# The mean of a group norm moved from the pixels into the biases of the products behind it

## The reference

```
x = x + attention(gn(x))     # 12 heads of 32, each pixel sees a 7x7 window and 16 registers
x = x + experts(gn(x))       # router over 4 experts, top 2, each 384 -> 96 -> 384 with gelu

gn(v):  g = v in 32 groups of 12 channels;  (g - mean) / sqrt(var + 1e-5), over all pixels of an image
attention(x): q, k, v = x @ qkv_w.T + qkv_b;  reg_k, reg_v = registers @ qkv_w[384:].T + qkv_b[384:]
              softmax(q . [k of the window, reg_k] / sqrt(32)) @ [v, reg_v] @ out_w.T + out_b
experts(x):   probs = softmax(x @ router_w.T + router_b), two largest, made to sum to 1 (weights c_e)
              sum over e of c_e * (gelu(x @ fc1_w[e].T + fc1_b[e]) @ fc2_w[e].T + fc2_b[e])
```

## Time and profile before

| | |
|---|---|
| median of 3 runs | 627.7 us (627.43 to 632.37) |
| profiled execution | 630.17 us, of which the span 628.4 |
| mean granted TensorE clock | 0.992 |
| instructions | 22407 |
| matmuls on TensorE | 9227 |
| VectorE, ScalarE, GpSimd instructions | 1009, 609, 427 |

### The profile page before, as it was taken

One profiled execution on the slowest core, in us unless ns is written; L12 is line 12 of the kernel. 1 busy time (PEld: TensorE's weight loads), 2 busy tenths in 40 slices (PEclk: granted clock), 3 DMA queues, 4 the chain that ended last, 5 costly groups with the idle time before them and its releaser, 6 DMA issues.

```text
span 628.4 us, 22407 instructions
## 1 busy us (share of the span) xinstructions
PE 564.3 (90%) x9227; PEld 389.5 (62%) x9227; DVE 449.1 (71%) x1009; ACT 307.5 (49%) x609; POOL 292.0 (46%) x427
## 2 busy tenths in 40 slices
PE   3668789999998999898899998997988899998998
PEld 2337666676765766566666776656666556665554
DVE  6885676886887689775778887875687797773233
ACT  1763455224643488523453246531786438644321
POOL 3106774372814856429573546325676322313131
PEclk9999999999999999899999999998998999999999
DMA  8869769794369852597537964588440001211212
GB/s 308 189 148 288 197 176 267 208 267 125 94 149 228 241 135 61 129 246 220 133 89 184 279 173 133 127 217 229 129 135 25 2 35 42 77 40 38 76 44 108
DMA packets 130637, 94.11 MB, mean 150 GB/s; under 512 B 67132, under 2 KB 124392, under 8 KB 130536
## 3 DMA queue, kind: packets, MB, share of 16 engines
q1 hardware_dynamic: 121896, 77.39, 46.3%
q0 software_dynamic: 8640, 15.30, 8.0%
HBM read 56.29 MB, written 35.54 MB: 146 GB/s over the span
## 4 chain that ended last, share of the span: by engine, by line
PE 60%; DVE 18%; DMA 7%; issue 6%; ACT 5%; SPq 2%; POOL 1%; ACTq 0%; DVEq 0%; POOLq 0%
PE ps L1168 41%; PE ps L1351 7%; PE ps L1328 4%; PE ps L1302 4%; DVE MX L675 3%; DMA QS<-MT 3%; DVE ST L459 2%; DMA KB<-kscr 2%; DVE ON L695 1%; DVE SUMT L688 1%; DVE RINV L694 1%; SPq L262 1%; DVE X L562 1%; DVE KT L537 1%; DMA X<-in_x 1%
## 5 line engine op out<-in xcount | busy, mean ns | idle before, releaser
L1168 PE MATMUL ps<-XH,WQ 128*128 128x384 f16 x810 | 148.5, 333 | 14.5 <-DVE XH L508 8.2
L675 DVE TENSOR_REDUCE MX<-ps 128x2 f32<-128x372 f32 x216 | 107.8, 538 | 36.5 <-PE ps L1302 34.5
L1168 PEld LDWEIGHTS ps<-XH,WQ 128*128 128x128 f16 x810 | 76.9, 99 | 68.9 <-issue 12.6
L983 ACT ACTIVATE PT<-ps 128x448 f32<-128x448 f32 (+1 forms) x162 | 78.9, 509 | 49.2 <-PE ps L1328 49.0
L439 POOL TENSOR_TENSOR KT<-QS,KT 128x384 f16<-128x384 f32 x36 | 34.3, 963 | 95.2 <-ACT KT L1081 95.2
L1302 PE MATMUL ps<-KB,QS 120*32 120x186 f16 x1728 | 63.5, 247 | 12.6 <-issue 3.6
L1328 PE MATMUL ps<-QS,KB 122*128 122x112 f16 (+1 forms) x864 | 61.0, 212 | 9.7 <-DMA QS<-MT 5.2
L1168 PE MATMUL ps<-WQ,XH 128*128 128x128 f16 x972 | 61.8, 221 | 4.0 <-issue 4.0
L1168 PE MATMUL ps<-OS,WO 128*128 128x384 f16 x324 | 61.7, 326 | 2.3 <-DVE X L551 1.5
L380 POOL DMA_DIRECT2D QS<-MT x72 | 38.2, 535 | 51.0 <-ACT MT L973 48.9
L1168 PEld LDWEIGHTS ps<-WQ,XH 128*128 128x128 f16 x972 | 55.3, 99 | 10.0 <-issue 7.8
(11 more groups left out here) (167 smaller groups left out, 971.9 us busy)
## 6 DMA issues: line engine op xcount, KB each, us to landing
KB<-kscr SPq DMA_DIRECT2D x108, 192.0 KB, 4.2
kscr<-KT SPq DMA_DIRECT2D x72, 192.0 KB, 2.6
VR<-vscr SPq DMA_DIRECT2D x216, 56.0 KB
QS<-qscr SPq DMA_DIRECT2D x108, 96.0 KB, 5.3
X<-in_x SPq DMA_DIRECT2D x12, 576.0 KB, 5.4
out<-X SPq DMA_DIRECT2D x11, 576.0 KB, 3.3
qscr<-QT POOLq DMA_DIRECT2D x18, 192.0 KB, 3.9
qscr<-PT POOLq DMA_DIRECT2D x18, 192.0 KB, 5.3
```

The lines of the kernel that those rows point to most:

```text
L675: V.tensor_reduce(out=MX[:, s % 2, t, 2 * pair:2 * pair + 2], in_=ps[:, S_BANK(s, i), 0:2 * RUN].rearrange("p (h n) -> p h n", h=2), op=AL ...
L983: A(PTS[n % 4][:, 0:w], ps[:, ST_BANK(n), 0:w], ACT.Exp, scale=SCORE).then_inc(s_["exd"], 1)
L1168: last = mm(bank, lhsT(a, k), rhs(b, k), start=(k == 0 and n == 0), stop=(finish and k == steps - 1 and n == 2))
```

## The change

The first half becomes x * rstd, without nb: the mean is no longer taken out of the pixels. Since every product behind the norm is linear, the missing part is a constant for each output channel, nb passed through the weights, and it is added to the biases instead:

- `normalised` on VectorE and the blocks for k = 2 on ScalarE go. The second half is x * rstd minus the first half, in one VectorE instruction (`scalar_tensor_tensor`). For n = 1 and 2, GpSimd keeps k = 0 alone, with two instructions (a scaling into GT_ and a subtraction); VectorE takes k = 1 and 2, in each column for the strip of the column before, and in column 5 for strip 5 too.
- GpSimd makes `shifted_registers(n)`: registers minus nb, with nb as a 17th column, in halves (four small operations). The registers are shifted the other way, since the key and value biases that they are given hold the shift for pixels.
- `registers(i)` now runs for both images, i = 0 to 5, and has 36 products: register keys with the key shift (17 columns), query shift and value shift (one column each), register values. i = 3 to 5 stand at the end of the queries phase of stage 2. New biases BQ, the value bias BVX and from it obx are made by VectorE (`bias_columns`, `value_columns`, `output_bias`); `value_bias` runs again in stage 3.
- The gelu bias is FBX, made from `hidden_shift` (27 products of one column, stage 5 and expert part); the router's bias gets `logit_shift` (9 products).
- To have nb earlier, the group means of stages 2 and 5 move from behind queries 2 to behind queries 1, `parameters`, `deviation` and `more_parameters` one step each.
- `register_values(gi)`, two transfers on GpSimd's queue, moves from behind the query outputs to ahead of them.

The diff, cut to its core (the first `low_half` is the one of GpSimd, the second the one of VectorE):

```diff
-POOL_K = ((), (0, 1, 2), (0, 1, 2), ())
+POOL_K = ((), (0,), (0,), ())
...
             def low_half(n, blk, k):
...
+                link(nc.gpsimd.tensor_scalar(tmp, x_block(n, blk, k), cols["rstd"][:, k:k + 1], None, ALU.mult))
                 pool.wait_ge(s_["gn_hi"], n * GN_STEPS + blk * KC + k + 1)
-                nc.gpsimd.tensor_tensor(xh_block(n, blk, 1, k), tmp_block(n, k), xh_block(n, blk, 0, k), ALU.subtract
-                                        ).then_inc(s_["gn_lo_p"], 1)
+                nc.gpsimd.tensor_tensor(xh_block(n, blk, 1, k), tmp, xh_block(n, blk, 0, k), ALU.subtract).then_inc(s_["gn_lo_p"], 1)
+
+            def shifted_registers(n):
+                pool.wait_ge(s_["gn_par"], n + 1)
...
+                nc.gpsimd.tensor_tensor(RGF[:, :, 0:REGS], cols["regs"].rearrange("p (k n) -> p k n", n=REGS),
+                                        cols["nb"].unsqueeze(2).broadcast_to([P, KC, REGS]), ALU.subtract)
+                link(nc.gpsimd.tensor_copy(RGF[:, :, REGS:RCOLS], cols["nb"].unsqueeze(2)))
+                link(nc.gpsimd.tensor_copy(RG[:, 0, :, :], RGF[:, :, :]))
+                nc.gpsimd.tensor_tensor(RG[:, 1, :, :], RGF[:, :, :], RG[:, 0, :, :], ALU.subtract).then_inc(s_["rg"], 1)
...
             for gi in range(STAGES):
+                if gi:
+                    register_values(gi)
                 for s in range(TILES):
                     queries_out(gi, s)
-                if gi:
-                    register_values(gi)
+                    if gi in (2, 5) and s == 4:
+                        shifted_registers(gi // KC + 1)
...
-                V.tensor_scalar(tmp_block(n, k), x_block(n, blk, k), cols["rstd"][:, k:k + 1], cols["nb"][:, k:k + 1],
-                                ALU.mult, ALU.add).then_inc(s_["gn_t"], 1)
...
             def low_half(n, blk, k):
-                V.tensor_tensor(xh_block(n, blk, 1, k), tmp_block(n, k), xh_block(n, blk, 0, k), ALU.subtract).then_inc(s_["gn_lo_v"], 1)
+                dve.wait_ge(s_["gn_hi"], n * GN_STEPS + blk * KC + k + 1)
+                V.scalar_tensor_tensor(out=xh_block(n, blk, 1, k), in0=x_block(n, blk, k), scalar=cols["rstd"][:, k:k + 1],
+                                       in1=xh_block(n, blk, 0, k), op0=ALU.mult, op1=ALU.subtract).then_inc(s_["gn_lo_v"], 1)
...
                     reciprocals(gi, 4)
                     if n:
-                        normalised(n, s, 0)
+                        low_halves(n, s - 1)
                     if more:
                         keys_low(gi + 1, 3)
+                    normalise(gi, 4)
                     if n:
-                        normalised(n, s, 1)
-                    normalise(gi, 4)
+                        low_halves(n, s)
...
-                    if gi in (2, 5) and s == 2:
+                    if gi in (2, 5) and s == 1:
                         parameters(gi // KC + 1, 0)
-                    if gi in (2, 5) and s == 4:
+                    if gi in (2, 5) and s == 3:
                         more_parameters(gi // KC + 1)
...
+                if gi == 2:
+                    bias_columns(1, 0, KC)
+                    value_columns(1)
+                    for i in range(KC, 2 * KC):
+                        register_low(i)
...
-                A(xh_block(n, blk, 0, k), x_block(n, blk, k), ACT.Identity, bias=cols["nb"][:, k:k + 1],
+                A(xh_block(n, blk, 0, k), x_block(n, blk, k), ACT.Identity, bias=cols["zero"],
...
+            def registers(i):
+                img, g = divmod(i, KC)
+                pe.wait_ge(s_["rg"], img + 1)
                 pe.wait_ge(s_["wlo"], g + 1)
...
+                split_product(ps[:, 0, at:at + RCOLS], lambda a, k: WQ[:, g, a, k, P:2 * P], lambda b, k: RG[:, b, k, :])
+                split_product(ps[:, 0, at + RCOLS:at + RCOLS + 1], lambda a, k: WQ[:, g, a, k, 0:P], shift)
+                split_product(ps[:, 0, at + RCOLS + 1:at + RCOLS + 2], lambda a, k: WQ[:, g, a, k, 2 * P:3 * P], shift)
+                split_product(ps[0:REGS, 0, at + 32:at + 32 + P], lambda a, k: RG[:, a, k, 0:REGS], lambda b, k: WQ[:, g, b, k, 2 * P:3 * P]
+                              ).then_inc(s_["kr_mm"], 1)
...
-                    if gi == 0:
-                        pe.wait_ge(s_["kr_lo"], KC)
-                        pe.wait_ge(s_["vr_sb"], KC)
+                    if gi in (0, 2) and i == 3:
+                        pe.wait_ge(s_["kr_lo"], KC * (gi // 2 + 1))
+                        pe.wait_ge(s_["vr_sb"], KC * (gi // 2 + 1))
+                        pe.wait_ge(s_["bvlo"], gi // 2 + 1)
...
-                    if gi in (2, 5) and s == 2:
+                    if gi in (2, 5) and s == 1:
                         group_means(gi // KC + 1, 0)
...
+                if gi == 2:
+                    for i in range(KC, 2 * KC):
+                        registers(i)
+                if gi == KC:
+                    value_bias(1)
+                if gi == 5:
+                    hidden_shift(0, 0, 0)
```

More of the change, by code:

```diff
@@ new lines, in low_halves, with bias_columns, value_columns @@
+            def low_halves(n, blk):
+                for k in range(KC):
+                    if k not in POOL_K[n]:
+                        low_half(n, blk, k)
+            def bias_columns(img, first, end):
+                dve.wait_ge(s_["kr_mm"], KC * img + end)
+                V.tensor_tensor(BQ[:, img, first:end, :], regs_ps[:, first:end, REGS:REGS + 2],
+                                cols["qkb16"].rearrange("p (g t) -> p g t", t=2)[:, first:end, :], ALU.add).then_inc(s_["bq"], 1)
+            def value_columns(img):
+                link(V.scalar_tensor_tensor(out=BVX[:, :], in0=regs_ps[:, :, REGS + 2], scalar=1 / WS, in1=cols["bv"],
+                                            op0=ALU.mult, op1=ALU.add))
+                link(V.tensor_copy(BVH[:, 0, :], BVX[:, :]))
+                V.tensor_tensor(BVH[:, 1, :], BVX[:, :], BVH[:, 0, :], ALU.subtract).then_inc(s_["bvlo"], 1)
@@ L820, in result @@
                                        op0=ALU.mult, op1=ALU.add).then_inc(s_["y_done"], 1)
-            def last_values(blk):
-                for k in range(2):
-                    normalised(3, blk, k)
             def last_lows(blk):
@@ L888, in _ @@
             weigh(15)
-            last_values(5)
             weigh(16)
@@ L999, in _ @@
                     if gi == 0:
-                        for k in range(2):
+                        for k in range(KC):
                             normalised(0, a, k)
-                        if dve_lows(0, a) > 0:
-                            act.wait_ge(s_["gn_lo_v"], dve_lows(0, a))
-                        A(tmp_block(0, 2), x_block(0, a, 2), ACT.Identity, bias=cols["nb"][:, 2:3], scale=cols["rstd"][:, 2:3]).then_inc(s_["gn_ta"], 1)
-                        normalised(0, a, 2)
                         if a == 0:
@@ L1204, in value_bias, with hidden_shift, logit_shift @@
                 last.then_inc(s_["bv_mm"], 1)
+            def hidden_shift(img, bank, at):
+                pe.wait_ge(s_["rg"], img + 3)
+                pe.wait_ge(s_["flo"], 1)
+                for j in range(KC):
+                    last = split_product(ps[:, bank, at + j:at + j + 1], lambda a, k: W1[:, a, k, j * P:(j + 1) * P], shift)
+                last.then_inc(s_["fb_mm"], 1)
+            def logit_shift():
+                split_product(ps[:, 5, RSPAN:RSPAN + EXPERTS], lambda a, k: shift(a, k).broadcast_to([P, P]), lambda b, k: RWs[:, b, k, :])
```

242 lines of the change are left out of this document (120 added, 122 removed).

## The result

The changed kernel took 644.5 us (median of four runs, 641.0 to 647.7), the one before 628.6 beside it: ratio 1.027, interval 1.021 to 1.032. That is slower by some 16 us, where 636.6 with a range of 629.5 to 643 was forecast: the sign is right, the size too small by half. The execution shown here is the fastest of the four, 641.01 us with 639.2 of span.

A forecast was written before the change was run, and what follows sets the result against it. The prediction took TensorE, busy 564 of 628.4 us, to bound the kernel, with other engines counting only where it waits for them. Its terms summed to +8.9 us on the 627.7 median: 636.6 us, range 629.5 to 643.

The forecast's parts named there:

- rival D: Clock falls behind two new waits for group means and one ending stage 2: 641.2 us, chance 0.10.
- c: Stages 2 and 5: group means moved one step ahead make TensorE wait, +3.0 us for both (1.6 to 4.6).
- e: End of stage 2: new wait before keys strip 4, old wait before strip 5 gone, -1.0 us (-3.1 to +2).
- a: Start: key strips come faster as VectorE does less, first keys come later, -2.0 us (0 to -3.6).
- b: Small register products added in two steps behind the queries of stage 0, +1.1 us.
- d: Stage 2: register products for image 1, their waits, less a covered wait, +4.7 us (2 to 7).
- f: Attention in stages 2 and 5: VectorE's two-SBUF-input operations held beside GpSimd, +1.0 us (0 to 6.2).
- rival C: SBUF sharing holds VectorE in full in attention of stages 2 and 5, 6.2 us: 641.8 us, chance 0.08.
- h: Stage 5: shift of the hidden layer behind a short wait, less a wait it covers, +0.2 us.
- i: Expert part: added small products and a link on the first router, freed VectorE blocks worthless, +1.6 us (0.6 to 1.6).
- Rival A: VectorE relief in attention of stages 2 and 5 is worth more, -7.7 us: 627.9 us, no change, chance 0.15.
- B: Rival: stage 2's register block hides as transfers hold attention, block cost about 0.7 us: 632.6 us, chance 0.13.

The follow-up runs named there:

- e1: Changed kernel with group means, parameters, deviation and reciprocal of stages 2 and 5 put back where the kernel before had them: 638.24 us, ratio 1.021.
- e3: Changed kernel with the nine products of queries 1 made twice in stages 2 and 5: 637.27 us, ratio 1.019.
- e13: Changed kernel with the group means of stages 2 and 5 put behind the first three output projections: 639.94 us, ratio 1.020.
- e12: Changed kernel with VectorE's second halves in the expert part moved behind the third weighing and a result: 644.07 us, ratio 1.026.
- e4: Changed kernel with the first key strip of stage 1 put ahead of stage 0's waiting key scores: 643.92 us, ratio 1.029.
- e2: Changed kernel with only 12 instead of 108 register products for image 1 in stage 2, results incomplete: 640.02 us, ratio 1.021.
- e0: Changed kernel run again, unedited, as the measure for other runs: 644.06 us, ratio 1.026.

## Why the prediction was too low, step by step

**The step that failed** is the clock. The prediction named it as rival D ("the clock falls behind the new waits of c (two) and e, each like the 1.25 above"), gave it 0.10 and 641.2, and priced c in the forecast by the wait alone. The rows that should have decided were in hand: behind the 1.90 us of the earlier trace rows the clock was at 0.50, and a new wait of 2.3 to 2.4 is longer than that one. The two waits of before that were longer than 2 us ended the same way (from its timeline, and the stretches behind them, with the clock ahead of the last two numbers):

```profile
433.15 1.48 PE L1168 MATMUL ps<-WQ,XH 128*128 128x128 f16 x19 [2.20 <-issue]
476.81 0.51 PE L1328 MATMUL ps<-QS,KB 122*128 122x88 f16 x8 [2.01 <-DMA QS<-MT]
```

```profile
434.00:437.00 3.00, 3.00 (x45) 2.50 (x43) 1.55 (x4) 0.88 (x2) 1.55 (x3) 0.50 0.66 199
478.50:481.50 3.00, 2.78 (x48) 2.16 (x48) 2.44 (x6) 2.42 (x6) 1.84 (x2) 0.50 0.02 5
```

The runs showed a loss of 1.7 us, in some profiles twice that, behind each such wait, in 13 of 16 cases; moreover falls at two places that D did not have: behind the register block (the 1.17 and 2.26 in place of 0.64 and 1.68, 1.1 us, and some 0.3 in the last products of the block) and behind the lengthened transfer of stage 0.

By terms:
- **a and b** (-2.0, +1.1): the sums right, the sixth strip 2.1 earlier and the way from it to the first scores 0.9 longer. Two parts of a were off and made up for each other: the strips gained 0.6 each, not 0.7 (3.32 to 2.73), and the first keys came only 0.27 later, not 0.8. The second half was mis-sized: three take 1.67 us, not 1.48, since one takes 0.61 where the subtraction took 0.55. VectorE still sets the pace of a strip, without idle time.
- **c** (+3.0): the mechanism and the wait right (2.34 less 0.82 is 1.5 in each stage), the size half. With the clock each stage loses 3.2; e1, e3 and e13 gave back 5.8, 6.8 and 7.0 us.
- **d** (+4.7): block 4.1 us (4.3), wait for the registers 0.39 (0.4), the 0.97 covered as said. The wait of 1.0 ahead of the fourth score group was 0 in the changed kernel, where slow products stood in its place, and 0.62 at full clock (e3). Sum right, one part replaced by the clock. In 8 of the 12 profiles with the block in a row, a stall of 0.6 to 1.4 us that no engine explains stood behind its first value product.
- **e** (-1.0): both waits came as forecast, 1.86 ahead of strip 4 (1.7), none ahead of strip 5, with full clock behind it: 27 products took 4.55, 1.6 less than the 6.14 of the earlier trace rows, where 0.8 had been counted. The 0.52 behind them was not forecast. Behind the 1.86 the clock fell in 4 of 16 profiles, as rival D had it.
- **f** (+1.0) and **rival C:** the holds came in another place. In stage 2's attention twelve second halves took 0.655 us on average, against some 0.61 unheld: 0.5 us of holds. In the expert part they took 0.90: GpSimd's subtraction held them, three in 3.02 against 1.67 unheld. The twelve that ran beside a subtraction of GpSimd took 1.05 on average and 1.30 at most, the six others 0.61; in the kernel before, thirteen such took 0.72. Of the Trainium skill's GPSIMD Engine Reference, section Specifications (SBUF interfaces shared with VectorE, contended by its instructions with two SBUF inputs), the runs so agree in the expert part, where the forecast had not applied it, and hardly in attention, where rival C had put it.
- **g** (+0.3): not resolved by a row. **h** (+0.2): the shift took 0.76 behind a wait of 0.46, less the 0.97 that it covers: right.
- **i** (+1.6): the products right, but "VectorE's freed blocks buy nothing" missed that the fused halves cost: 2.1 us of TensorE's waits for results instead of 0.5 (e12 gives back 1.4 of them).
- **Not in the forecast:** stage 0's transfer, 1.2 to 2.7 us more of wait in the unedited profiles and those of e1 to e3. It is issued among the same transfers (the load of image 1, the value windows), 0.89 us later than before, and the products that wait for it start 2 us later; that it shares the engines with them is argued, not shown. An edit of the order (e4) shortens the wait.

Rival A did not happen: from the first key scores to the last, attention of stage 2 took 43.3 us against 40.8, and that of stage 5 37.2 against 38.9, the latter with the 2.01 us wait shown above in it. B was refuted: the block lay fully on TensorE's path (e2: 4.0 us).

## What to carry to other kernels

A wait of TensorE is priced with what runs behind it: look up in the rows of before at which granted clock the products behind waits of that length ran, and add that to the forecast itself, with its share of cases (here 28 of 35 for waits of 2.3 us or more), not to a rival. Filling a wait can then pay even with work that nobody needs; here nine products made twice, in two places, gained 6.8 us (0.7% by the ratios). Fusing two VectorE operations into one with two SBUF inputs is not half the price: here it cost 0.61 us against 0.48 and 0.55, and 1.05 on average beside GpSimd's subtraction in the expert part.

## What the runs showed of the hardware that was not expected

- The clock fell behind 108 small products in which TensorE was busy by the records throughout (27 of 17 columns and one in 0.83 us, nine of 128 in 0.67): in 8 of 12 profiles, and in none of three where the same products stood in three groups between scores and values. Fifteen profiles are few for that, and in e0 the fall came together with a stall of 1.41 us. The Trainium skill's TensorE: Matmul & The Clock Gate, section HAM oscillation — how this bites in real kernels, describes the other case, in which waits for transfers between products bring the clock down again and again; the waits of stage 0 agree (3.79 us, then eight products in 2.13 instead of 1.47).
- Stalls that no engine explains stand at places fixed in the instruction stream: at 62 to 64 us in every profile of the changed kernel and its variants (1.3 to 1.8 us), at 432 to 433 in both profiles of the old stream (2.20 and 2.14). The change moved them; in sum they did not grow (10.8 us before, 5.8, 6.3 and 8.4 in the changed kernel).
- Low clocks are drawn anew in each execution: the same kernel lost 10.2, 11.9 and 17.1 us to them in three profiles, so one profile of a kernel does not settle a difference of a few microseconds.
